# Re-placing the side work of an interleaved attention loop, and the bank pairs of the shared feed-forward

## The chip, the cores and the metric

The kernel is one decoder layer written in Bass for one NeuronCore of a Trainium2 chip. It runs on one core. The metric is the device time of one execution in microseconds. Every engine (TensorE, called PE in the profile; VectorE, DVE; ScalarE, ACT; GpSimd, POOL; SyncE, SP) has a program of its own, in a fixed order written out by hand, and the five programs meet only at semaphores.

## The reference

Input is `x` (16 batches, 128 tokens, 256 features) and a context of the same shape. Three residual blocks follow each other:

```
x = x + attn(layernorm(x))          # differential attention, 16 heads x 2 halves of 8, two softmaxes, o = a1 - lam*a2,
                                    # rms norm over each head's 16 values, times subln_w, @ W_proj + b_proj
x = x + xattn(layernorm(x), ctx)    # softmax((q Wq+bq)/8 . (ctx Wk+bk)) @ (ctx Wv+bv), @ Wf + bf, gelu, + ctx
x = x + ffn(layernorm(x))           # shared: (silu(x w1) * (x w2)) w3, hidden 1024
                                    # routed: sigmoid router, top 2 of 16 experts of hidden 256, gates times outputs
```

All of it is float32; only the attention's scores use three-part bfloat16 splits.

## The kernel before, in words

The 16 batches are four chunks of four (`NC = 4`, `CB = 4`). The program has these stages:

- **Head.** Loads, the first layernorm, and `qk`/`values` of chunks 0 and 1. Queries and keys are split into three bfloat16 parts (`put_first` on ACT, `subtract_first` on DVE, `put_second` on ACT, `put_third` on POOL), stored to HBM by `store_part`, and fetched back in packed form by `fetch`.
- **The attention loop**, `STEPS = 32` steps of two halves `(s, a)`. A half is, on PE: `exps(s, a)` (8 matmuls, line 428, banks 2 and 3), `scores(s + 3, a)` (8 matmuls, line 407, banks 0 and 1), one `pv` (line 440, bank 4), in the second half also `turn_max(s + 2)` (line 415, bank 5), and then `between(s, a)`. DVE takes the maximum of the scores (`max_of`, line 875), and once a step turns the outputs (line 882) and takes reciprocals (line 886). ACT does the exponentials (line 1348) and copies the turned maxima (line 1341). POOL splits the maxima (`split_max`, lines 1589 to 1595) and combines the outputs (`combine`, lines 1604 to 1613). SP sends the maxima into the query tile (`put_max`, line 1790); `exps(s, 0)` waits for that transfer (`m_put`).
- **Pieces between the halves.** Everything else that can be done early is hung into the loop by tables that name a half `(s, a)`: `qk` and `values` of chunks 2 and 3, the folding of the cross attention's weights (WF, A, B, M), the turned context, keys and values of the cross attention (CTX, KEYS, U), the attention's output projection with its norm (CLIP, SQUARE, SUM, ROOT, NORM, OT, OUT, ADD), the next layernorm (STATS, SCALE, NORMAL, ROWS), and the cross attention of chunks 0 and 1 (SCORES, MAX, EXP, TURN_P, WEIGH, FO). Each engine's own `between` looks its part up in the tables. The pieces share PSUM banks 6 and 7, so a piece waits until the one before it in its bank has been read.
- **After the loop.** Cross attention of chunks 2 and 3 among the first `up`s of the shared feed-forward; `up(c, f)` computes 128 hidden columns of gates and ups for chunk c (line 612), `silu_up` and `gate_up` make `hTs`, and `down(c, j)` multiplies by `W3s` (line 623). Routing (`route`) runs on DVE in between: `chosen_both`, a matmul that ranks, `slotted`. POOL then scatters the rows to expert slots (line 1729).
- **Experts.** 47 tiles (`turn_x`, `raise_`, `lower`), rows scattered back by line 1632.
- **End.** The shared `up`s 2 to 7 of chunk 3, the routed rows added (lines 1132, 1135), `down(3, j)`, and the output.

The order on SP is fixed as well: in step s it does `put_max(s + 2)`, then the packed fetches, stores and context loads of that step. SP waits at each instruction in turn.

## Time and profile before

| | us |
|---|---|
| median of 3 runs | 595.57 (593.27 to 596.82) |
| the profiled execution, time | 595.6 |
| its span, first to last instruction | 594.4 |
| PE busy in the span | 541.0 (91%) |
| DVE busy | 311.4 (52%) |
| ACT busy | 261.2 (44%) |
| POOL busy | 229.5 (39%) |
| mean granted TensorE clock | 0.974 of full speed |

The profiled execution lies at the median of the runs; 1.2 us of its time lie outside the span. A row of a timeline is: start, duration, engine, line, operation, what it writes and reads, count, and in brackets how long the engine stood idle before it and what ended that. PE's granted clock falls after idle stretches, and then the same matmuls take about twice as long.

### The profile page before, as it was taken

How to read it: one execution, taken by the hardware profiler on the slowest of the kernel's cores; microseconds unless marked ns; L12 is line 12 of the kernel's file. 1: busy time of each engine (PE TensorE's matmuls, PEld its weight loads, DVE VectorE, ACT ScalarE, POOL GpSimd, SP SyncE). 2: the span in 40 equal slices, each digit the busy share in tenths (PEclk: the TensorE clock that was granted, in tenths of full speed). 3: DMA queues.
4: the chain of work that ended last, by engine and by line, in shares of the span. 5: the costliest groups of instructions: out<-in, count | busy, mean ns of one | idle time of the engine just before them, and what ended most of it. 6: DMA issues, size and time to landing. Idle time of an engine off the chain costs nothing.

```text
span 594.4 us, 10885 instructions
## 1 busy us (share of the span) xinstructions
PE 541.0 (91%) x3792; PEld 372.6 (63%) x3792; DVE 311.4 (52%) x677; ACT 261.2 (44%) x420; POOL 229.5 (39%) x473
## 2 busy tenths in 40 slices
PE   8968879689887879899999899999999999999888
PEld 6544435355544544665685457456999999999347
DVE  5867865957796797896242752111222222222184
ACT  6326555444562554835412200201666666665110
POOL 2534775635553554422010004563243334443100
PEclk9989998989897999999999989999999999999899
DMA  7892562713222141990029906222233333332552
GB/s 241 230 204 74 152 193 78 229 53 112 81 67 74 42 145 59 150 285 1 0 71 350 288 0 195 90 89 71 73 91 94 95 93 96 91 90 76 198 187 72
DMA packets 62197, 72.46 MB, mean 122 GB/s; under 512 B 14816, under 2 KB 55264, under 8 KB 60608
## 3 DMA queue, kind: packets, MB, share of 16 engines
q1 hardware_dynamic: 58160, 60.59, 36.0%
q0 software_dynamic: 3792, 10.39, 5.0%
q10 hardware_dynamic: 192, 0.79, 0.6%
q8 instruction: 32, 0.52, 0.4%
q14 instruction: 21, 0.17, 0.1%
HBM read 45.32 MB, written 26.03 MB: 120 GB/s over the span
## 4 chain that ended last, share of the span: by engine, by line
PE 49%; issue 18%; DVE 13%; POOL 10%; DMA 5%; ACT 3%; SPq 2%; POOLq 0%; DVEq 0%; ACTq 0%
PE ps L612 17%; PE ps L623 9%; POOL y_rows L1632 7%; DVE nmax L875 3%; PE ps L539 3%; PE ps L440 2%; PE ps L376 2%; PE ps L389 2%; PE ps L428 2%; DVE OT L882 2%; PE ps L407 2%; PE ps L505 2%; PE ps L520 2%; POOL goes_to L1626 1%; PE ps L632 1%
## 5 line engine op out<-in xcount | busy, mean ns | idle before, releaser
L875 DVE TENSOR_REDUCE nmax<-ps 128x8 f32<-128x1024 f32 x64 | 77.7, 1215 | 43.4 <-PE ps L407 39.4
L668 PE MATMUL ps<-xt,Wn 128*128 128x128 f32 x752 | 91.8, 275 | 0.3 <-ACT xt L1450 0.3
L668 PEld LDWEIGHTS ps<-xt,Wn 128*128 128x128 f32 x752 | 87.7, 192 | 0.6 <-ACT xt L1450 0.5
L1348 ACT ACTIVATE prob<-ps 128x1024 f32<-128x1024 f32 x64 | 65.5, 1023 | 35.9 <-PE ps L428 35.9
L1632 POOL DMA_INDIRECT y_rows<-yo,goes_to x47 | 46.0, 978 | 81.8 <-DVE yo L1129 81.5
L1443 ACT ACTIVATE sil<-ps 128x512 f32<-128x512 f32 x32 | 19.1, 597 | 122.1 <-PE ps L612 119.3
L1121 DVE TENSOR_TENSOR ht<-sa,ps 128x256 f32<-128x256 f32 x47 | 19.8, 421 | 99.2 <-PE ps L679 95.2
L612 PE MATMUL ps<-xT,W1s 128*128 128x512 f32 x128 | 63.7, 622 | 3.5 <-DVE yo L1129 1.9
L623 PE MATMUL ps<-W3s,hTs 128*128 128x256 f32 x256 | 56.5, 381 | 4.4 <-DVE hTs L1052 4.4
L612 PE MATMUL ps<-xT,W2s 128*128 128x512 f32 x128 | 60.3, 593 | 0.0
L1052 DVE TENSOR_TENSOR hTs<-sil,ps 128x512 f32<-128x512 f32 x32 | 21.9, 686 | 70.1 <-PE ps L612 66.0
L623 PEld LDWEIGHTS ps<-W3s,hTs 128*128 128x128 f32 x256 | 48.2, 190 | 14.0 <-DVE hTs L1052 5.9
L1729 POOL DMA_INDIRECT x_slots<-XN,slot_i x32 | 31.9, 996 | 62.3 <-DVE slot_i L1102 43.1
L1463 ACT ACTIVATE Wn<-W 128x1024 f32 x47 | 49.7, 1057 | 12.6 <-issue 12.6
L679 PE MATMUL ps<-W,ht 128*128 x188 | 48.3, 380 | 0.2 <-DVE yo L1129 0.2
L440 PE MATMUL ps<-prob,Vp 128*32 128x256 f32 x512 | 42.2, 402 | 4.0 <-DVE OT L882 2.8
L612 PEld LDWEIGHTS ps<-xT,W2s 128*128 128x128 f32 x128 | 24.5, 192 | 31.6 <-issue 30.2
L612 PEld LDWEIGHTS ps<-xT,W1s 128*128 128x128 f32 x128 | 24.3, 197 | 29.1 <-issue 25.6
L428 PEld LDWEIGHTS ps<-pack_q,pack_k 51*128 51x128 bf16 x512 | 15.1, 95 | 36.4 <-issue 25.9
L1604 POOL TENSOR_SCALAR rden<-rden,neg_lam 128x8 f32<-128x8 f32 x32 | 11.9, 371 | 67.3 <-DVE rden L886 67.3
L428 PE MATMUL ps<-pack_q,pack_k 51*128 51x128 bf16 x512 | 26.1, 222 | 10.8 <-ACT prob L1348 7.7
L407 PE MATMUL ps<-pack_k,pack_q 48*128 48x128 bf16 x512 | 25.9, 221 | 10.8 <-DVE nmax L875 6.5
(186 smaller groups left out, 854.6 us busy)
## 6 DMA issues: line engine op xcount, KB each, us to landing
W<-in_L_ffn_routed_w_dram SPq DMA_DIRECT2D x12, 1024.0 KB
pack_q<-qk_parts SPq DMA_DIRECT2D x48, 128.0 KB, 3.1
xg<-x_slots SPq DMA_DIRECT2D x47, 129.0 KB
x_slots<-zero SPq DMA_DIRECT2D x11, 512.0 KB, 10.3
pack_k<-qk_parts SPq DMA_DIRECT2D x42, 128.0 KB, 3.1
qk_parts<-part SPq DMA_DIRECT2D x21, 256.0 KB, 3.1
yg<-y_rows SPq DMA_DIRECT2D x4, 1024.0 KB, 8.6
X<-in_x_dram SPq DMA_DIRECT2D x4, 512.0 KB, 7.0
```

What stands on the lines that cost most here:

```text
L407: r = t.matmul(ps[:, b + m, h * P:(h + 1) * P], Qp[u][rr, 4 * a + h, lo:lo + P], Kp[u][rr, 4 * a + h, lo:lo + P], start=True, stop=True, t ...
L428: r = t.matmul(ps[:, 2 + m, h * P:(h + 1) * P], Kp[u][rr, 4 * a + h, lo:lo + P], Qp[u][rr, 4 * a + h, lo:lo + P], start=True, stop=True, t ...
L440: r = t.matmul(ps[VP * h:VP * (h + 1), 4, a * 2 * P:(a + 1) * 2 * P], Vp[:, s // CS % 2, s % CB, s // CB % 2 * HU + 4 * a + h, :], prob[:, ...
L612: r = t.matmul(ps[:, up_bank(c, f) + i, :], w[:, k, f * P:(f + 1) * P], xT3[c][:, k, :], start=(k == 0), stop=(k == KT - 1))
L623: r = t.matmul(ps[:, 2 + j % 2, 0:D], hTs[:, f, j * P:(j + 1) * P], W3s[:, f, :], start=(f == 0), stop=(f == FS - 1))
L668: r = t.matmul(ps[:, 2 + p, h * P:(h + 1) * P], Wn[:, n % 3, k, h * P:(h + 1) * P], xt[:, p, k, :], start=(k == 0), stop=(k == KT - 1))
L679: r = t.matmul(ps[:, 6 + p, 0:D], ht[:, p, k, :], W3[:, ds(e, 1), k, :].rearrange("p o f -> p (o f)"), start=(k == 0), stop=(k == KT - 1))
L875: v.tensor_reduce(nmax[:, s % 4, a, :, :], ps[:, b:b + 2, :].rearrange("p m (h t) -> p m h t", h=4), AX_X, ALU.max, negate=True).then_inc( ...
L1348: a.activation(prob[:, n:n + 2, :], ps[:, 2:4, :], ACT.Exp, scale=HD ** -0.5).then_inc(exped, 1)
L1463: a.activation(Wn[:, n % 3, :, :].rearrange("p k f -> p (k f)"), W12[:, ds(e, 1), :, :].rearrange("p o k f -> p (o k f)"), ACT.Copy).then_ ...
L1632: g.indirect_dma_start(out=y_rows, out_offset=bass.IndirectOffsetOnAxis(ap=goes_to[:, n:n + 1].bitcast(U32), axis=0), in_=yo[:, p, :], in_ ...
L1729: g.indirect_dma_start(out=x_slots, out_offset=bass.IndirectOffsetOnAxis(ap=slot_i[:, i, b:b + 1].bitcast(U32), axis=0), in_=XN[:, b, :], ...
```

## The change

All of the tables that place pieces are new. Several pieces are divided in two or four: `root_o` (2 parts to 4), `norm_o`, `turn_attn`, `add_o`, `stats` and `put_fo` (1 to 2 each). `project_values(2, i)` moves from behind the loop into it. The first two `values(1, i)` come before the first `scores`, and DVE takes six maxima in a row. The load of context chunk 1 goes to a tile of its own (`Cx1`, over weights no longer needed), no longer waits for the stores of chunk 3, and is loaded a second time at step 16 for the residual. On SP, a context load now comes ahead of `put_max` of its step; the eight loads of `Wp` are split over steps 5 and 6. Each piece waits for the reader of its bank that the new tables make the last one. In the shared feed-forward, chunks 2 and 3 use two pairs of banks in turn, one `up` of the next chunk goes ahead of each chunk's `down`s, one `up` goes ahead of the ranking matmuls, and the last `up`s no longer wait for the last expert tile's output (`y_put`) but for its input (`xt_put`).

```diff
-TURN_AT = (2, 1)
-QK_AT = ((3, 0), (4, 0), (5, 0), (6, 0))
-VALUES_AT = {2: ((8, 0), (8, 1)), 3: ((16, 0), (16, 1))}
-WF_AT, A_AT, B_AT, M_AT = (1, 0), (1, 1), (7, 0), (7, 1)
-CTX_AT = {0: (9, 1), 1: (11, 1), 2: (17, 0), 3: (28, 0)}
+STATS3_AT, SCALE3_AT, NORM3_AT, TURN_AT = (0, 0), 0, (1, 1), (2, 0)
+QK_AT = ((3, 0), (4, 0), (7, 0), (9, 0))
+VALUES_AT = {2: ((9, 1), (11, 0)), 3: ((18, 1), (19, 1))}
+WF_AT, A_AT, B_AT, M_AT, PUT_B_AT, WP_AT = (5, 0), (1, 0), (10, 0), (8, 0), (11, 1), (9, 0)
+CTX_AT = {0: (12, 0), 1: (12, 1), 2: (20, 0), 3: (26, 0)}
...
-STATS_AT = {0: (14, 1), 1: (23, 0), 2: (31, 0)}
-SCALE_AT = {0: 15, 1: 23, 2: 31}
-CONTEXT_AT = {0: 17, 1: 25}
-CTX_LOAD_AT = {0: 4, 1: 10, 2: 12, 3: 16}
+STATS_AT = {0: ((16, 1), (18, 0)), 1: ((24, 0), (24, 1)), 2: ((30, 1), (31, 0))}
+SCALE_AT = {0: 18, 1: 25, 2: 29}
+CONTEXT_AT = {0: (29, 29, 29, 29), 1: (30, 30, 31, 31)}
+CTX_LOAD_AT = {0: 4, 1: 11, 2: 15, 3: 20}
+CTX1_AGAIN_AT = 16
...
         def up_bank(c, f):
-            return 4 if c == NC - 1 and f < AHEAD else 0
+            if c == NC - 1:
+                return 4 if f < AHEAD or f % 2 else 0
+            return 4 if c == NC - 2 and f % 2 == 0 else 0
+
+        def down_bank(c, j):
+            return 2 + j if c == NC - 1 else 2 + j % 2
...
+            for i in range(2):
+                values(1, i)
             scores(0, 0)
-            values(1, 0)
             scores(0, 1)
-            values(1, 1)
+            turn(norm, 2, 4, xn)
             scores(1, 0)
-            turn(norm, 2, 4, xn)
...
-            for i in range(2):
-                project_values(2, i, 6 + i)
             t.wait_ge(o_turned, STEPS)
...
-            for f in (3, 4, 5):
+            for f in (3, 4, 5, 6):
                 up(1, f)
             t.wait_ge(chosen_both, 1)
...
-            t.wait_ge(y_put, NT)
+            t.wait_ge(xt_put, NT)
             for f in range(AHEAD, FS):
                 up(NC - 1, f)
...
             for s in range(STEPS):
+                for c in range(NC):
+                    if s == CTX_LOAD_AT[c]:
+                        if c == 1:
+                            q.wait_ge(a_made, 1)
+                            q.wait_ge(b_made, 1)
...
+                        fetch_context(c)
                 if s + LEAD - 1 < STEPS:
                     put_max(s + LEAD - 1)
```

On PE, just ahead of the loop, the order before was as follows (L407 are the first scores, L389 `values(1, i)`, L362 the turn of chunk 2, L415 `turn_max`, L376 `qk(2, i)`, L428 the first `exps`):

```order
L407 MATMUL ps<-pack_k_81,pack_q_78 128x128 x8
L389 MATMUL ps<-Wv__95,xT 128x256 x4
L407 MATMUL ps<-pack_k_81,pack_q_78 128x128 x8
L389 MATMUL ps<-Wv__95,xT 128x256 x4
L407 MATMUL ps<-pack_k_81,pack_q_78 128x128 x8
L362 MATMUL ps<-ident,xn 128x128 x8
L407 MATMUL ps<-pack_k_81,pack_q_78 128x128 x8
L415 MATMUL ps<-identb,mpart 128x128
L407 MATMUL ps<-pack_k_81,pack_q_78 128x128 x8
L376 MATMUL ps<-xT_99,Wqk 128x512 x2
```

The same place on PE in the changed kernel (L416 are `values`, L434 scores, L381 the turn, L442 `turn_max`, L399 `qk`):

```order
L416 MATMUL ps<-Wv__95,xT 128x256 x8
L434 MATMUL ps<-pack_k_81,pack_q_78 128x128 x16
L381 MATMUL ps<-ident,xn 128x128 x8
L434 MATMUL ps<-pack_k_81,pack_q_78 128x128 x8
L442 MATMUL ps<-identb,mpart 128x128
L434 MATMUL ps<-pack_k_81,pack_q_78 128x128 x8
L399 MATMUL ps<-xT_99,Wqk 128x512 x2
```

Both `values` now stand ahead of the first scores, and the first two scores follow each other.

On SP, steps 4 to 6 of the loop before (the packed fetches read `qk_parts`, the stores write it, `mT` is `put_max`):

```order
L1790 DMA pack_q_79<-mT 3x8x128 x2
L1782 DMA pack_q_78<-qk_parts 16x4096 x4
L1758 DMA qk_parts<-part_108 128x2x512 x4
L1794 DMA Cx<-in_ctx_dram 128x4x256
L1790 DMA pack_q_79<-mT 3x8x128 x2
L1782 DMA pack_q_78<-qk_parts 16x4096 x2
L1782 DMA pack_k_81<-qk_parts 16x4096 x2
L1790 DMA pack_q_80<-mT 3x8x128 x2
L1782 DMA pack_k_81<-qk_parts 16x4096 x4
```

And SP in steps 4 to 6 of the changed kernel:

```order
L1897 DMA Cx<-in_ctx_dram 128x4x256
L1893 DMA pack_q_79<-mT 3x8x128 x2
L1885 DMA pack_q_78<-qk_parts 16x4096 x4
L1861 DMA qk_parts<-part_108 128x2x512 x4
L1893 DMA pack_q_79<-mT 3x8x128 x2
L1885 DMA pack_q_78<-qk_parts 16x4096 x2
L1885 DMA pack_k_81<-qk_parts 16x4096 x2
L1853 DMA Wp<-in_L_attn_W_proj_dram 16x2x256 x4
L1893 DMA pack_q_80<-mT 3x8x128 x2
L1885 DMA pack_k_81<-qk_parts 16x4096 x4
L1853 DMA Wp<-in_L_attn_W_proj_dram 16x2x256 x4
```

The context load went from behind the stores to the front, and the `Wp` loads came into these steps.

On POOL, the end of the loop before, from the last `split_max` (`rden`, `o` and `Ob` are one `combine`, `y` the layernorm's scale, `sq` the clip):

```order
L1595 TENSOR_TENSOR mpart<-mrest,mpart 128x2x2x4
L1604 TENSOR_SCALAR rden<-rden,neg_lam 128x2x4
L1607 TENSOR_TENSOR o_92<-OT,rden 128x128 x2
L1613 TENSOR_TENSOR Ob<-o_92 128x2x4x16
L1604 TENSOR_SCALAR rden<-rden,neg_lam 128x2x4
L1607 TENSOR_TENSOR o_92<-OT,rden 128x128 x2
L1613 TENSOR_TENSOR Ob<-o_92 128x2x4x16
L1604 TENSOR_SCALAR rden<-rden,neg_lam 128x2x4
L1607 TENSOR_TENSOR o_92<-OT,rden 128x128 x2
L1613 TENSOR_TENSOR Ob<-o_92 128x2x4x16
L1568 TENSOR_SCALAR y<-mv 128x4
L1570 TENSOR_TENSOR y<-y,minus_half 128x4
```

And POOL at the end of the changed loop, from the `combine` of step 28:

```order
L1701 TENSOR_SCALAR rden<-rden,neg_lam 128x2x4
L1704 TENSOR_TENSOR o_92<-OT,rden 128x128 x2
L1710 TENSOR_TENSOR Ob<-o_92 128x2x4x16
L1665 TENSOR_SCALAR y<-mv 128x4
L1667 TENSOR_TENSOR y<-y,minus_half 128x4
L1738 TENSOR_TENSOR X<-X,Cx 128x256 x4
L1701 TENSOR_SCALAR rden<-rden,neg_lam 128x2x4
L1704 TENSOR_TENSOR o_92<-OT,rden 128x128 x2
L1710 TENSOR_TENSOR Ob<-o_92 128x2x4x16
L1738 TENSOR_TENSOR X<-X,Cx 128x256 x2
```

The scale, which needs DVE's statistics of step 31, and the context additions now stand ahead of the `combine`s of steps 29 to 31.

## Rows read from the trace of the kernel before

**Rows 1.** Stages (the windows view): stretch, length, busy of each engine, PEclk, DMA.
```profile
49.26:100.84 51.58, 45.65 (x515) 24.83 (x515) 37.22 (x57) 30.25 (x48) 34.46 (x82) 0.97 0.45 136
100.84:242.09 141.25, 117.00 (x1318) 67.51 (x1317) 108.61 (x195) 72.78 (x116) 71.84 (x200) 0.94 0.36 95
242.09:254.61 12.52, 10.95 (x68) 9.57 (x64) 11.69 (x30) 9.89 (x22) 5.88 (x10) 1.00 1.06 207
```
**Rows 2.** Timeline of PE: one half with a piece, one without, the next `exps`.
```profile
75.14 0.40 PE L428 MATMUL ps<-pack_q,pack_k 51*128 51x128 bf16 x8 [0.92 <-ACT prob L1348]
76.27 1.99 PE L376 MATMUL ps<-xT,Wqk 128*128 128x512 f32 x4
78.18 0.40 PE L428 MATMUL ps<-pack_q,pack_k 51*128 51x128 bf16 x8
80.46 0.40 PE L428 MATMUL ps<-pack_q,pack_k 51*128 51x128 bf16 x8 [0.93 <-ACT prob L1348]
```
**Rows 3.** The page's group of the loop's exponentials on ACT.
```profile
L1348 ACT ACTIVATE prob<-ps 128x1024 f32<-128x1024 f32 x64 | 65.5, 1023 | 35.9 <-PE ps L428 35.9
```
**Rows 4.** Timeline of PE, three long waits in the loop.
```profile
87.06 0.40 PE L428 MATMUL ps<-pack_q,pack_k 51*128 51x128 bf16 x8 [2.20 <-DMA pack_q<-mT]
120.56 1.97 PE L496 MATMUL ps<-ident,Cx 128*128 128x128 f32 x8 [4.63 <-DMA Cx<-in_ctx_dram]
150.26 0.40 PE L407 MATMUL ps<-pack_k,pack_q 48*128 48x128 bf16 x8 [1.30 <-DVE nmax L875]
```
**Rows 5.** Timeline of PE: the first scores, the first `exps`.
```profile
34.66 0.40 PE L407 MATMUL ps<-pack_k,pack_q 48*128 48x128 bf16 x8 [4.09 <-DMA pack_q<-qk_parts]
49.26 0.40 PE L428 MATMUL ps<-pack_q,pack_k 51*128 51x128 bf16 x8 [0.72 <-DMA pack_q<-mT]
```
**Rows 6.** Timeline of SP's queue.
```profile
46.34 4.46 SPq L1790 DMA_DIRECT2D pack_q<-mT  x4
76.77 2.69 SPq L1782 DMA_DIRECT2D pack_q<-qk_parts  x4
82.72 1.59 SPq L1790 DMA_DIRECT2D pack_q<-mT  x2
94.70 3.68 SPq L1750 DMA_DIRECT2D Wp<-in_L_attn_W_proj_dram  x8
```
**Rows 7.** Timeline of POOL at the loop's end, and one context addition.
```profile
215.48 0.72 POOL L1639 TENSOR_TENSOR X<-X,Cx 128x256 f32<-128x256 f32 x1
243.64 0.32 POOL L1604 TENSOR_SCALAR rden<-rden,neg_lam 128x8 f32<-128x8 f32 x1
245.48 1.56 POOL L1621 TENSOR_SCALAR sq<-Ob 128x1024 f32<-128x1024 f32 x1
```
**Rows 8.** Timeline of PE in the shared feed-forward.
```profile
341.51 0.70 PE L788 MATMUL ps<-both,earlier 128*128 128x256 f32 x2 [2.22 <-DVE before L1081]
352.29 14.08 PE L623 MATMUL ps<-W3s,hTs 128*128 128x256 f32 x64 [0.88 <-DVE hTs L1052]
```
**Rows 9.** The chain of waits, the eight `up`s of chunk 2: start, us, what.
```profile
366.37 27.48 PE ps L612 x64
```
**Rows 10.** Timelines of DVE, POOL and PE: routing, and the first expert tile.
```profile
354.18 0.17 DVE L1102 CAST slot_i<-top 128x16 int32<-128x16 f32 x1
412.28 0.19 POOL L1626 CAST goes_to<-xg 128x1 int32<-128x1 f32 x1 [3.69 <-DMA xg<-x_slots]
415.47 0.60 PE L657 MATMUL ps<-ident,xg 128*128 128x128 f32 x4
```
**Rows 11.** Timelines of PE and SP's queue at the end.
```profile
553.74 3.64 PE L612 MATMUL ps<-xT,W1s 128*128 128x512 f32 x4 [1.87 <-DVE yo L1129]
556.38 2.27 SPq L1906 DMA_DIRECT2D yg<-y_rows  x4
577.98 14.08 PE L623 MATMUL ps<-W3s,hTs 128*128 128x256 f32 x64 [1.68 <-DVE hTs L1052]
```
**Rows 12.** The tile view of `yg`: its DMA from issue to landing.
```profile
DMA to landing us min/median/max: 5.2/8.6/11.8
```

More of the change, by code:

```diff
@@ L501, in project_keys @@
                 t.wait_ge(cT_put, 2 * (c + 1))
-                if c == 2 and e:
-                    t.wait_ge(kT_put, KT * 2 + 1)
+                if c == 0 and e == 0:
+                    t.wait_ge(a_put, 1)
+                if (c, e) == (0, 0):
+                    t.wait_ge(cT_put, 4)
+                if (c, e) == (1, 0):
+                    t.wait_ge(x_added, 1)
+                if (c, e) == (1, 1):
+                    t.wait_ge(cT_put, 6)
+                if (c, e) == (2, 0):
+                    t.wait_ge(norm.put, 10)
+                if (c, e) == (2, 1):
+                    t.wait_ge(u_put, 4)
                 for k in range(KT):
@@ L605, in up @@
                 n = FS * c + f
+                left = n - 1 if c >= NC - 2 and (c, f) != (NC - 1, 1) else n
                 if f == 0:
@@ L700, in tensor_program @@
                 qk(1, i)
+            for i in range(2):
+                values(1, i)
             scores(0, 0)
-            values(1, 0)
             scores(0, 1)
-            values(1, 1)
+            turn(norm, 2, 4, xn)
             scores(1, 0)
-            turn(norm, 2, 4, xn)
-            scores(1, 1)
             t.wait_ge(identb_made, 1)
@@ L712, in tensor_program @@
             turn_max(0)
+            scores(1, 1)
+            qk(2, 0)
             scores(2, 0)
-            qk(2, 0)
+            turn_max(1)
             scores(2, 1)
-            turn_max(1)
             qk(2, 1)
@@ L772, in tensor_program @@
             t.wait_ge(u_put, 2 * NC)
-            down(0, 0)
             weigh_values(3)
             route_logits(2)
-            for j in range(1, CB):
+            for j in range(CB):
                 down(0, j)
@@ L1209, in vector_program @@
             root_o(0)
+            root_o(1)
             gate_up(0, 0)
-            root_o(1)
+            root_o(2)
+            root_o(3)
             put_logits(0)
-            norm_o(NC - 1)
-            turn_attn(NC - 1)
+            for i in range(2):
+                norm_o(NC - 1, i)
+            for i in range(2):
+                turn_attn(NC - 1, i)
             gate_up(0, 1)
             normalize(norm3, 1, 1, rows(XN, 1))
-            put_fo(2)
-            add_o(NC - 1, 4)
+            for i in range(2):
+                put_fo(2, i)
+            for i in range(2):
+                add_o(NC - 1, i)
             v.wait_ge(x_added, 2 * NC)
@@ L1233, in vector_program @@
             gate_up(0, 7)
-            put_fo(3)
+            for i in range(2):
+                put_fo(3, i)
             put_logits(2)
@@ L1649, in between @@
                     put_third(2, 3)
-                if (s - 1, 0) in QK_AT:
-                    put_third(3, QK_AT.index((s - 1, 0)))
+                for i in range(4):
+                    if s == THIRD_AT[i]:
+                        put_third(3, i)
                 for c in range(NC - 1):
@@ L1854, in sync_program @@
                         store_part(2, i)
-                if s == 7:
-                    for j in range(4):
+                if s in (5, 6):
+                    for j in (0, 1) if s == 5 else (2, 3):
                         for i in range(2):
```

448 lines of the change are left out of this document (263 added, 185 removed).

## The prediction

> **What bounds the kernel now.** I read the slices of the page first (PE near nine tenths all the way, with dips between 50 and 250 us), then the windows of the stages, then PE's timeline half by half, and for every idle stretch of PE its releaser on DVE, SP and POOL. The stages are in [rows 1]: steps 0 to 8 of the loop take 51.58 us with PE busy 45.65, steps 9 to 31 take 141.25 with PE busy 117.00 at a granted clock of 0.94, the way from the loop to the first shared `up` 12.52. So PE bounds the loop, but not tightly: about 30 us of the loop are PE idle, and more is lost because the matmuls behind an idle stretch run at the lower of the two clock levels. DVE is busy 108.61 of the 141.25, unevenly.
>
> An ordinary half is in [rows 2]. From `exps` to piece 1.13 us (75.14 to 76.27), the piece 1.91, so 3.04 in all. The half without a piece lasted 2.28 with 0.93 of PE idle, since the next `exps` need the exponential out of banks 2 and 3. That takes 1.02 [rows 3]; with 0.4 for `exps` and what is between them an empty half costs at least about 1.6 on an even course. A piece in an otherwise empty half is therefore nearly half free, and a half in which DVE has more than PE is lost.
>
> The long waits are in [rows 4]: 2.20 for the maxima's transfer, 4.63 for context chunk 1, 1.30 for a late maximum; three more of 1.35, 1.19 and 0.98 are of the same kind.
>
> **Part 1, ahead of the loop.** PE stands 4.09 us until the packed queries land at 34.66 [rows 5], and then does two `values` of 1.9 us between the first scores, which makes DVE's six maxima wait. After the change both `values` fit into the 4.09. Then the chain is DVE's: six maxima of 1.22 in a row with one late score give about 43.9, the two `qk` end at 44.1. The first maxima's transfer can be issued at about 39.3; in [rows 6, 5] from issue (46.34) to the first `exps` (49.26) it is 2.9, so 42.2, not late. `exps` at 44.1 instead of 49.26: **-5.2** (bounds -3, if `turn_max` is late by a piece, and -6).
>
> **Part 2, steps 0 to 8.** For every half I added up what stands there on PE, DVE and ACT at these durations, and took the largest, or 1.6. Before, 13 pieces lie in these steps and the sum is 47.8, against 51.58 measured. After, 9 pieces lie there and the sum is 42.1. But SP does not get shorter. In steps 4 to 6 of the new order stand, between one `put_max` and the next, a fetch of 2.69, stores and context load, which took until 82.72 together [rows 6], and now half of the `Wp` loads (3.68 for eight) twice: 6.5, 5.9 and 5.9 us of issue, while the halves of steps 5 and 6 ask for only 3.2 to 3.6 a step. Following the queue through: the transfer for step 7 is issued some 6.5 us after that for step 6 and lands 2.9 to 4.3 later (4.3 is 82.72 to 87.06 in [rows 6, 4]), so `exps(7, 0)` waits 2.5 to 3.9, and steps 4, 5, 6, 8 and 9 some 0.5 to 1.3 each. I take 5.1 for all: 47.2, **-4.4** (bounds -9.5, no backlog, and -1).
>
> What the page on DMA says bears on this. The Trainium skill ("DMA: Bandwidth & Descriptors", section "Issuing engines are not separate DMA queues") has it that the time a sequencer takes to initiate a DMA is usually small beside the DMA. Here it is not: four issues took 2.69 us [rows 6]. By that rule there would be no backlog and this part would be worth the -9.5 that stand above as a bound.
>
> **Part 3, steps 9 to 31.** Same sum: before 134.2 with 32 pieces, after 128.2 with 38, because the loads that DVE has beyond PE's in its heavy halves fall from 21.6 to 7.5 us (norm, transposition, root, sums and `put_fo` divided, layernorm later). Before, 141.25 less the six long waits and their slow matmuls (about 16.3) leaves 125.0, so 43% of DVE's surplus was absorbed by neighbours; after, by the same share, 128.2 - 3.2 = 125.0. The context load for chunk 1 is now issued behind a `put_max`, a fetch and stores of step 10, some 5.7 us into step 11, and needs 4.1; its piece stands 8.2 us in: a wait of 1.5 and a few slow matmuls, +2.0, in place of 4.63 and some. Each added wait on a bank I followed to its reader: it stands a half or more ahead, so nothing for those; +3.0 for what such a count does not see. 130.0, **-11.3** (bounds -16 and -5). Two `project_values` are in this sum.
>
> **Part 4, from the loop to the first `up`.** This gets longer. POOL's scale of chunk 2 is placed at step 29 but needs DVE's statistics of step 31. Behind it on POOL stand four context additions of 0.72 [rows 7], the `combine` of step 29 (1.65), two additions, a `combine`, two more, and the `combine` of step 31. DVE's last turn of the outputs waits for the `combine` of step 29. Counted from the end of the statistics: scale 1.4, additions to 4.3, `combine` to 6.0, so the last turn starts at 6.0 and the normalisation of chunk 2 at 7.0; before it came at 1.5. The last `pv` ends at 3.1, and PE, whose `project_values` are gone from here, stands idle about 4 us. The clip (1.56, [rows 7]) ends at 13.8 and the first `up` starts at about 19.1, so 16.0 after the last `pv` against 12.52 [rows 1]; the matmuls behind the idle stretches add 1.5. **+5.0** (bounds 0 and +8).
>
> **Part 5, feed-forward.** Each `up` takes 3.43 (27.48 for eight, [rows 9]). PE waits 2.22 for `chosen_both` and then runs the ranking and an `up` slowly [rows 8]: from 339.1 to 366.2 it takes 27.1 for two `up`s, 1.0 of ranking and 14.08 of `down`, which is 21.9. With an `up` ahead of the ranking and one ahead of the `down`s, all 5.2 go; the waits of 0.88 and 0.94 for `hTs` go likewise at the next two chunk ends: 0.85 and 0.94. The two bank pairs themselves are worth nothing between these: 27.48 for eight is PE without a gap. Is the first tile there? Slot numbers are ready at 354.35 and the tile has landed at 412.3, needed at 415.47 [rows 10]. Slots come 4.4 us earlier, since DVE no longer waits behind slow `up`s; the tile then lands 1.7 before PE comes, 6.0 earlier than before. At the end PE waits 1.87 for the last output copy and then runs slowly (3.64, full speed 1.9) [rows 11]; both go, 3.6. The routed rows land 5.2 us after the issue at 556.38 at the earliest [rows 12], by 561.6; DVE needs them from 562.9, has eight additions ahead of the last `hTs` instead of eleven, and the wait of 1.68 [rows 11] falls to 0.8. Together 0.9 + 6.0 + 4.6: **-11.5** (bounds -12.5 and -7).
>
> **Sum.** -5.2 - 4.4 - 11.3 + 5.0 - 11.5 = -27.4. From the span of 594.4 that is 567.0, and with the 1.2 us outside it **568.2** against 595.6 of the profiled execution, which is the median of the runs.
>
> **Rivals.**
> - *SP's backlog does not bite, or the tail is short* (parts 2 or 4 at their good bound): 568 - 5 = 563. For it: before, with 95% of these issues in the same order, only one wait of 2.20 is seen. Against: those steps lasted 4.6 to 5.4 us then. 18%.
> - *SP's queue holds the loop further on*: late landings of 4.3 us throughout, the context chunk 1 behind them, parts 2 and 3 at -1 and -7: 568 + 8 = 576. For it: the fetches, stores and second context load are all still there in less time. 22%.
> - *The tile chain takes the feed-forward's gain*: if the scatter is not earlier, PE waits for the first tile at step six of its gain, part 5 is -7: 573. 8%.
> - *Slower than before*, by one mechanism, the clock in steps 9 to 31: if each of the many small waits leaves PE at the lower level, a piece costs about 3.6 to 3.7 instead of 1.9 (the ratio in [rows 11]). From about 16 of the 38 pieces at that level the 27 us are used up; all give 568 + 67. Before, about five pieces ran so, each behind a wait of over a microsecond. 4%, at about 600.
> - *The gain is not there*, since the pieces only swap waits: within 0.5%, 3%.
>
> **Chances and range.** My forecast, between 564 and 573, has 45%. The 8-in-10 range goes from the good rival's lower side to the bad one's upper: **558 to 582**. Within 0.5% (3 us) cannot be told from no change here. Faster 0.93, same 0.03, slower 0.04.
>
> **What would show it.** Part 1: first `exps` at 43 to 46. Part 2: a wait of 2 us or more for the maxima's transfer at `exps(7, 0)`, step 9 at 90 to 93. Part 3: the wait for context chunk 1 down to 1 to 2 us, PE's clock in the stage above 0.96. Part 4: POOL's context additions directly behind the scale, PE idle some 4 us, 15 to 18 us from the last `pv` to the first `up`. Part 5: no wait at the ranking, and `up`s directly behind the last `lower`. The prediction is wrong if the loop is not at least 10 us shorter, or if new waits on bank readers add up to over 5 us.

## The result, and the profile after

The changed kernel takes **567.8 us** (median of 4 runs, 566.11 to 569.25) against 594.42 (4 runs) of the kernel before beside it: ratio 0.956, 95% interval 0.949 to 0.964. Forecast was 568.2. Its profiled execution took 569.25, the slowest of the four, with a span of 568.0; the stages below are of that one execution.

The windows view cut at the same places as [rows 1] (first `exps`, step 9, last `pv`, first `up`, first expert tile, last `lower`), the columns as there, without the experts' 136.4 us, which are the same in both; first the changed kernel:

```profile
46.20:94.22 48.02, 40.56 (x482) 20.35 (x481) 36.53 (x55) 29.05 (x45) 31.59 (x82) 0.93 0.48 146
94.22:223.89 129.67, 122.72 (x1365) 73.67 (x1365) 107.87 (x199) 75.48 (x122) 69.07 (x192) 0.97 0.44 110
223.89:240.56 16.67, 10.46 (x50) 8.75 (x49) 13.88 (x34) 7.82 (x19) 11.48 (x21) 0.80 1.11 292
240.56:393.80 153.24, 152.35 (x558) 96.00 (x559) 64.94 (x175) 38.33 (x61) 43.72 (x57) 1.00 0.37 119
...
530.18:568.00 37.82, 34.67 (x112) 20.84 (x111) 20.32 (x43) 3.58 (x6) 1.91 (x2) 1.00 0.50 177
```

and the two stages of the kernel before that answer to its last two:

```profile
254.61:415.47 160.86, 155.07 (x558) 96.54 (x559) 65.03 (x174) 38.34 (x61) 44.72 (x58) 0.99 0.41 129
...
551.86:594.40 42.54, 36.65 (x113) 21.70 (x112) 20.24 (x43) 3.59 (x6) 1.92 (x2) 0.96 0.44 158
```

| stretch | before | forecast | after | moved (forecast) |
|---|---|---|---|---|
| start to first `exps` | 49.26 | 44.1 | 46.20 | -3.1 (-5.2) |
| steps 0 to 8 | 51.58 | 47.2 | 48.02 | -3.6 (-4.4) |
| steps 9 to 31 | 141.25 | 130.0 | 129.67 | -11.6 (-11.3) |
| last `pv` to first `up` | 12.52 | 17.5 | 16.67 | +4.2 (+5.0) |
| first `up` to first tile | 160.86 | 154.0 | 153.24 | -7.6 (-6.9) |
| experts | 136.39 | 136.4 | 136.38 | 0 |
| last `lower` to the end | 42.54 | 37.9 | 37.82 | -4.7 (-4.6) |
| span | 594.40 | 567.0 | 568.00 | -26.4 (-27.4) |

What PE waits for in the changed kernel, from the list of waits (us in all, times, longest):

```profile
PE ps L455 <- DMA pack_q<-mT: 4.8, 5, 1.7
...
PE ps L381 <- DVE xn L920: 4.6, 1, 4.6
PE ps L529 <- DMA Cx<-in_ctx_dram: 2.1, 1, 2.1
PE ps L442 <- POOL mpart L1692: 1.9, 1, 1.9
```

Of the three long waits of [rows 4] shorter ones are left: the context chunk's wait is 2.1 for 4.63. Two are new. The maxima's transfer is late five times (four of them, at steps 6 to 9, are the backlog of part 2; the fifth, 1.12, is at step 17), and 4.6 us are lost in one place behind the loop (part 4). The last row is one that the forecast lacks, in the head; PE's timeline there:

```profile
38.27 0.27 PE L442 MATMUL ps<-identb,mpart 128*128 128x128 bf16 x1 [1.93 <-POOL mpart L1692]
39.01 3.78 PE L399 MATMUL ps<-xT,Wqk 128*128 128x512 f32 x4
44.02 2.25 PE L399 MATMUL ps<-xT,Wqk 128*128 128x512 f32 x4
46.20 0.40 PE L455 MATMUL ps<-pack_q,pack_k 51*128 51x128 bf16 x8
```

The gap of 4.09 of [rows 5] is gone, but `turn_max(0)` waits 1.93 us for POOL's split of the maxima, and the `qk` behind it runs at half speed, 3.78 for 1.98. The wait and the half speed are two things, as run 2 shows below: with the same wait of 1.93 its matmuls stay at full speed, and its first `exps` come at 43.50.

SP's queue in steps 4 to 6 (`put_max` is L1893, fetch L1885, stores L1861, `Wp` L1853), which answers to [rows 6]:

```profile
72.18 1.47 SPq L1893 DMA_DIRECT2D pack_q<-mT  x2
73.76 2.45 SPq L1885 DMA_DIRECT2D pack_q<-qk_parts  x4
76.25 2.19 SPq L1861 DMA_DIRECT2D qk_parts<-part  x4
78.49 1.60 SPq L1893 DMA_DIRECT2D pack_q<-mT  x2
...
82.67 2.44 SPq L1853 DMA_DIRECT2D Wp<-in_L_attn_W_proj_dram  x4
85.16 1.60 SPq L1893 DMA_DIRECT2D pack_q<-mT  x2
```

From one `put_max` to the next are 6.3 and 6.7 us; 6.5 and 5.9 were forecast. Behind the loop, on POOL, DVE and PE:

```profile
220.76 0.23 POOL L1665 TENSOR_SCALAR y<-mv 128x4 f32<-128x4 f32 x1 [11.16 <-DVE mv L908]
222.08 2.77 POOL L1738 TENSOR_TENSOR X<-X,Cx 128x256 f32<-128x256 f32 x4
```
```profile
224.96 0.18 DVE L1119 RECIPROCAL den<-den 128x4 f32<-128x4 f32 x1 [4.29 <-POOL X L1738]
226.75 0.70 DVE L956 STREAM_TRANSPOSE OT<-ps 128x512 f32<-128x512 f32 x1
227.92 1.83 DVE L920 TENSOR_SCALAR xn<-X,mv,y 128x256 f32<-128x256 f32 x4 [0.18 <-issue]
```
```profile
228.48 2.02 PE L381 MATMUL ps<-ident,xn 128*128 128x128 f32 x8 [4.59 <-DVE xn L920]
240.56 1.98 PE L671 MATMUL ps<-xT,W1s 128*128 128x512 f32 x4 [0.74 <-ACT xT L1397]
```

POOL waits 11.16 us in the scale, then does four context additions before its next `combine`. The normalisation starts 7.25 us after the statistics (220.67); 7.0 was counted.

In the feed-forward the waits of [rows 8] and the first wait of [rows 11] are gone: the ranking stands directly behind an `up`, the last `up`s directly behind the last `lower`, and of 1.68 ahead of the last `down`s 0.85 is left.

```profile
327.32 0.59 PE L857 MATMUL ps<-both,earlier 128*128 128x256 f32 x2
530.01 1.88 PE L671 MATMUL ps<-xT,W1s 128*128 128x512 f32 x4
551.62 14.08 PE L682 MATMUL ps<-W3s,hTs 128*128 128x256 f32 x64 [0.85 <-DVE hTs L1141]
```

### The profile page after: what moved, and what is told of

It is laid out like the page before. It is cut to its first block, busy times and chain, and to the rows that moved or that the text cites. A ratio compares the mean times of both kernels' runs of the same rounds, so it can differ in the third digit from the quotient of the medians.

```text
span 568.0 us, 10919 instructions
## 1 busy us (share of the span) xinstructions
PE 537.7 (95%) x3792; PEld 374.1 (66%) x3792; DVE 311.8 (55%) x685; ACT 260.1 (46%) x420; POOL 228.0 (40%) x473
## 4 chain that ended last, share of the span: by engine, by line
PE 80%; DVE 6%; SPq 5%; ACT 3%; issue 3%; DMA 2%; POOL 1%; ACTq 0%; DVEq 0%; POOLq 0%
PE ps L671 18%; PE ps L739 15%; PE ps L682 10%; PE ps L750 7%; PE ps L399 5%; PE ps L467 3%; PE ps L595 3%; PE ps L416 2%; PE ps L455 2%; PE ps L572 2%; PE ps L548 2%; SPq L1885 2%; DVE nmax L949 2%; PE ps L695 2%; PE ps L728 2%
## 5 line engine op out<-in xcount | busy, mean ns | idle before, releaser
L739 PE MATMUL ps<-xt,Wn 128*128 128x128 f32 x752 | 91.8, 275 | 0.1
L671 PE MATMUL ps<-xT,W1s 128*128 128x512 f32 x128 | 60.6, 596 | 1.6 <-ACT sil L1542 0.9
L399 PE MATMUL ps<-xT,Wqk 128*128 128x512 f32 x64 | 34.6, 684 | 1.6 <-ACT xT L1397 1.6
L750 PEld LDWEIGHTS ps<-W,ht 128*128 128x128 f32 x188 | 32.2, 191 | 3.1 <-issue 0.6
```

The source lines that it names most:

```text
L399: r = t.matmul(ps[:, qk_bank(c, i), :], Wqk[:, k, f, :, :].rearrange("p d m -> p (d m)"), xT_of(c)[:, k, :], start=(k == 0), stop=(k == KT ...
L671: r = t.matmul(ps[:, up_bank(c, f) + i, :], w[:, k, f * P:(f + 1) * P], xT3[c][:, k, :], start=(k == 0), stop=(k == KT - 1))
L739: r = t.matmul(ps[:, 2 + p, h * P:(h + 1) * P], Wn[:, n % 3, k, h * P:(h + 1) * P], xt[:, p, k, :], start=(k == 0), stop=(k == KT - 1))
L750: r = t.matmul(ps[:, 6 + p, 0:D], ht[:, p, k, :], W3[:, ds(e, 1), k, :].rearrange("p o f -> p (o f)"), start=(k == 0), stop=(k == KT - 1))
```

## The experiments

Each run's time is a median beside runs of the kernel before on its chip; since these differ a little from chip to chip (591.6 to 594.8), the ratio is the better measure. The changed kernel has 0.956 (0.949 to 0.964). Where times lie closer than about 3 us, the profiles are compared stage by stage. But a profile is one execution, and it too varies where an edit changes nothing: over the profiles of kernels with the changed kernel's loop from step 9 on (runs 1 to 4 and the changed kernel), steps 9 to 31 take 125.6 to 129.7 us; over those with its loop end, the way from the last `pv` to the first `up` takes 16.1 to 17.6.

**1. The feed-forward of the kernel before in the changed kernel** (`e1_ffn_before`).

```diff
-            for f in (3, 4, 5, 6):
+            for f in (3, 4, 5):
                 up(1, f)
...
-            up(1, 7)
-            up(2, 0)
+            for f in (6, 7):
+                up(1, f)
             for j in range(CB):
                 down(1, j)
...
-            t.wait_ge(xt_put, NT)
+            t.wait_ge(y_put, NT)
```

> The changed kernel with the shared feed-forward of the kernel before (order of ups and downs, one bank pair per up, the wait for the last output copy, the spread of the routed additions). My theory (part 5, all of it comes from matmuls put beside the waits): the waits for chosen_both, for hTs at two chunk ends and for the last output copy come back with their slow matmuls, 153.2 us from the first up to the first expert tile become 160.9, 37.8 us behind the last lower become 42.5, in all +12.3: about 580. Rival (the gain came from somewhere else, as transfers that no longer collide with the feed-forward's start): the stretches stay within 2 us of the changed kernel's, 568 to 571.

579.21 us, ratio 0.976 (0.971 to 0.981): +11.4. The windows of the two stretches:

```profile
238.71:398.38 159.67, 154.84 (x558) 96.41 (x559) 65.37 (x176) 38.32 (x61) 44.59 (x58) 0.99 0.37 118
535.07:577.50 42.43, 36.64 (x112) 21.70 (x112) 20.23 (x43) 3.58 (x6) 1.91 (x2) 0.96 0.45 158
```

The waits are back at their old size (2.21 at the ranking, 0.88, 0.85, 1.87, 1.68) and with them 6.4 + 4.6 us. That the gain of part 5 lies in this block is shown; the run puts the whole block back, so what each move in it is worth is read from its wait and was not tried singly. The missing 0.9 of the 12.3 is the wait of 0.94 for `hTs` of chunk 0, which did not come back. It stands ahead of this block: the changed kernel also has `weigh_values(3)` and `route_logits(2)` ahead of `down(0, 0)`, where the kernel before had them behind it, and this run leaves that as it is.

**2. SP's queue: the loads of `Wp` ahead of the loop** (`e4_wp_in_head`); the block of steps 5 and 6 moves ahead of `store_part(1, 0)`.

```diff
+            for j in range(4):
+                for i in range(2):
+                    load(Wp[...], W_proj..., head_weights_in)
             store_part(1, 0)
...
-                if s in (5, 6):
-                    (the same loads)
```

> The changed kernel with the eight loads of the projection's weights issued ahead of the loop (where SP's queue has 3.8 us free, 27.6 to 31.4) and not in steps 5 and 6. Theory (SP's issue time is what makes the maxima's transfers late in steps 6 to 9): the waits of 0.83, 0.79, 0.41 and 1.68 us before the exps of steps 6 to 9 shrink to under 1 in all, the slow matmuls behind them (1.1, 1.5, 1.5 us over full speed in steps 6, 7 and 9) go, steps 0 to 8 take 43.5 to 45 instead of 48.0: 563 to 565. Rival (the transfers are late because of their flight, 2.9 to 4.3 us, whatever is ahead of them in the queue): the waits stay above 3 us in all and the time within 1 us of 567.8.

566.28 us, ratio 0.953 (0.949 to 0.958), short of the 563 to 565 forecast. Step 9 starts at 91.83 instead of 94.22, since the wait of 1.68 there is gone. In the eight profiles with the changed kernel's list on SP for steps 0 to 9 it starts between 93.5 and 95.8, so this run is outside them and the `Wp` loads cost step 9 some 2 to 4 us. The stage itself is no shorter (48.33), as the loop began at 43.50. That earlier start does not come from the edit, which leaves PE's order in the head as it was: the wait is the same, only the matmuls behind it are fast.

```profile
38.10 0.22 PE L442 MATMUL ps<-identb,mpart 128*128 128x128 bf16 x1 [1.93 <-POOL mpart L1692]
38.57 1.98 PE L399 MATMUL ps<-xT,Wqk 128*128 128x512 f32 x4
43.50 0.40 PE L455 MATMUL ps<-pack_q,pack_k 51*128 51x128 bf16 x8
```

The largest wait is now at step 7:

```profile
71.32 3.15 SPq L1885 DMA_DIRECT2D pack_q<-qk_parts  x4
74.51 2.20 SPq L1861 DMA_DIRECT2D qk_parts<-part  x4
76.76 1.60 SPq L1893 DMA_DIRECT2D pack_q<-mT  x2
```
```profile
79.64 0.61 PE L455 MATMUL ps<-pack_q,pack_k 51*128 51x128 bf16 x8 [2.16 <-DMA pack_q<-mT]
```

The transfer for step 7 stands behind a fetch and four stores, not behind `Wp`. So `Wp` costs at step 9, and the stores of step 4 at step 7.

**3. Both `qk` of chunk 2 ahead of `turn_max`** (`e5_qk_first`).

```diff
+            qk(2, 0)
             turn_max(0)
             scores(1, 1)
-            qk(2, 0)
             scores(2, 0)
+            qk(2, 1)
             turn_max(1)
             scores(2, 1)
-            qk(2, 1)
```

> The changed kernel with both query-key projections of chunk 2 ahead of the transposition of the maxima that they followed, in the head. Theory (the head came out 2.1 us longer than forecast because PE waits 1.93 us for the first maxima and both projections behind that wait run at the lower clock level, 3.78 and 2.25 us instead of 1.98): the wait falls below 0.5, the projections take 2.0 each, first exps at 42.5 to 43.5 instead of 46.2, the rest unchanged: about 565. Rival (the maxima's chain on DVE and the transfer's flight set the first exps): first exps not before 45.5, the time within 1 us of 567.8.

569.13 us, ratio 0.958 (0.953 to 0.963). The wait is gone and the projections take 1.96 and 1.98, as the theory has it, but the whole gains nothing:

```profile
43.29 0.40 PE L455 MATMUL ps<-pack_q,pack_k 51*128 51x128 bf16 x8 [1.41 <-DVE nmax L949]
```
```profile
43.29:94.85 51.56, 43.29 (x481) 21.30 (x483) 36.99 (x55) 28.82 (x44) 31.23 (x82) 0.87 0.49 146
```

First `exps` 2.9 us earlier, at 43.29, but step 9 at 94.85: nothing of it is left. All four profiles with this order have their first `exps` at 43.2 to 43.5, behind a wait of 1.41 for a maximum of DVE; the nine with the old order have the wait of 1.93 to 1.94 and lie anywhere from 43.5 to 46.5. So the edit buys an even start, and against the best case of the old order almost nothing. Over the eight profiles of kernels with this list on SP for steps 0 to 9, the first `exps` lie between 43.3 and 46.5 and step 9 between 93.5 and 95.8, and the one that begins first is not the one that arrives first. In the changed kernel SP's queue is full from 57.4 to 97.5 us but for one gap of 0.4, so it sets step 9. Its length is not fixed, however: the 52 issues from `put_max(3)` to `put_max(9)` took 34.0 us in the changed kernel and 36.7 in this run, where four single issues lasted 1.19 to 1.63 instead of the usual 0.4 to 0.9; the other six lie between. What makes an issue long stays open.

**4. SP's list evened** (`e9_sp_even`, and `e10_sp_even_qk` with the edit of 3 as well).

```diff
-                if s in (3, 4):
-                    for i in ((0,), (1, 2))[s - 3]:
-                        store_part(2, i)
+                if s == 3:
+                    store_part(2, 0)
+                if s == 7:
+                    for i in (1, 2):
+                        store_part(2, i)
```

> The changed kernel with the projection's weights loaded ahead of the loop and the second and third parts of chunk 2's split stored at step 7 of SP's program instead of step 4 (four issues of 2.2 us; step 7 has none else). The runs so far have step 9 at 94 to 95 us whether the loop starts at 43.3 or at 46.2, and at 91.8 without the weights' loads. Theory (SP's queue, full without a gap from step 3 to step 7, sets the time of step 9, and the stores of step 4 are what makes the transfer for step 7 late): the waits before the exps of steps 6 to 9 fall below 1 us in all, step 9 at 87.5 to 90, the time 561 to 564. Rival (what is late is the transfer's own flight of 4 us while other transfers are on the way): waits of 2 us and more stay at steps 6 or 7, step 9 not before 91.5, the time within 1 us of the 566.3 measured with the weights moved alone.

> The same, and both query-key projections of chunk 2 ahead of the transpositions of the maxima in the head, which alone brought the first exps to 43.3 and the whole nothing (569.1 against 567.8). Theory (that gain was given back at SP's queue): with the queue relieved it stays, and the time is another 1 to 2 us under the run without it. Rival (the order of the head gives nothing whatever the queue is, because the idle time only moves to the wait for the maxima): within 0.7 us of that run.

563.92 (0.950, 0.945 to 0.955) and 562.72 (0.951, 0.946 to 0.956), on the same chip. Step 9 comes at 91.72 and 90.03, and steps 0 to 8 take 46.6 in both profiles, for 48.0. The waits for transfers at steps 7 to 9 are gone, as the theory has it. In these two profiles the earlier start of the second (43.47 for 45.15) is still there at step 9; but the first is of the slowest of its four executions and the second of the fastest, and the medians (1.2 apart, each with a spread of 4.6 or more) do not settle whether the head's order gains anything. The first is later at step 9 than the 87.5 to 90 I expected, and hardly earlier than in run 2, because at step 6 the rival is right: there the transfer leaves right behind a context load, and `exps` starts 4.3 us after its issue:

```profile
71.86 0.47 SPq L1897 DMA_DIRECT2D Cx<-in_ctx_dram  x1
72.38 1.48 SPq L1893 DMA_DIRECT2D pack_q<-mT  x2
```
```profile
76.72 0.61 PE L455 MATMUL ps<-pack_q,pack_k 51*128 51x128 bf16 x8 [2.23 <-DMA pack_q<-mT]
```

**5. The scale of chunk 2 at step 31** (`e2_scale_31`).

```diff
-SCALE_AT = {0: 18, 1: 25, 2: 29}
+SCALE_AT = {0: 18, 1: 25, 2: 31}
```

> The changed kernel with POOL's scale of chunk 2 at step 31 instead of 29, nothing else. In the changed kernel it waits 11.16 us on POOL for DVE's statistics of step 31, and four context additions, a combine, and on DVE the outputs put_fo(1) (whose buffer lies over chunk 0's context) and the last turn are late behind it; PE idles 4.59. Theory of the prediction, part 4 (the scale is what blocks POOL): the additions move ahead of the statistics, put_fo(1) starts as its matmuls end (223.3 counted in the changed kernel's time), the normalisation 2 us earlier, PE idle 2.6 and the first up 14 to 15 us after the last pv instead of 16.7: 565 to 566. Rival (DVE's own order sets the normalisation, the outputs and the last turn ahead of it): under 0.7 us of change in that stretch.

565.95 us, ratio 0.955 (0.950 to 0.960). The medians cannot tell this from the changed kernel, the profile can: PE waits 2.00 instead of 4.59, and the first `up` comes 14.52 us after the last `pv` instead of 16.67, where the kernels with the old placing have 16.1 to 17.6. That is as reckoned: what blocks POOL is the scale.

```profile
223.83 1.99 PE L381 MATMUL ps<-ident,xn 128*128 128x128 f32 x8 [2.00 <-DVE xn L920]
```

**6. The loop's end reordered** (`e11_tail`): context additions at steps 21 to 28, the scale of chunk 2 at step 30, and on DVE

```diff
+            normalize(norm, NC + 2, 2, xn)
+            for i in range(2):
+                put_fo(1, i)
             turn_o(STEPS - 1)
             invert(STEPS - 1)
-            normalize(norm, NC + 2, 2, xn)
             add_cross(0)
```

and on PE `project_values(3, i)` ahead of `cross_scores(2)`.

> The changed kernel with its loop end reordered: context additions at steps 21 to 24, 27 and 28, scale of chunk 2 at step 30, on DVE the normalisation of chunk 2 ahead of the outputs and the last turn, on PE the last project_values ahead of the cross scores. Theory (PE's idle 4.6 us and the slow matmuls behind it come from this order, not from a lack of work): xn is there when the last pv ends, the wait of 4.59 falls below 0.5, the first up comes 10.5 to 12 us after the last pv instead of 16.7: 562 to 563. Rival (POOL's combine of step 31, the clip and the scale of the next normalisation hold the first up at the same time after the loop): PE idles later in the same stretch instead, the first up not before 14.5 us, the time not under 565.5.

571.07 us, ratio 0.963 (0.958 to 0.967): slower than the changed kernel. The theory is wrong. The rival's numbers came in (first `up` 15.89 us after the last `pv`, PE idle later in the same stretch), but not for its reason:

```profile
228.00 1.11 PE L381 MATMUL ps<-ident,xn 128*128 128x128 f32 x8 [2.57 <-DVE OT L956]
228.93 5.30 PE L572 MATMUL ps<-M_T,cT 128*128 128x256 f32 x16
...
238.80 1.84 PE L381 MATMUL ps<-ident,XN 128*128 128x128 f32 x8 [2.78 <-DVE XN L920]
```

`xn` is ready in time, but the turn goes into the outputs' bank and so waits for DVE's last turn, which I had put behind the outputs; and DVE's queue has `max_cross` ahead of the next normalisation, so the cross scores, moved back behind `project_values(3, i)`, hold it up. The stretch is even 0.8 shorter than in the changed kernel; what is lost in this profile lies in steps 0 to 8 (49.2 for 48.0, within what this list on SP shows elsewhere) and behind the first `up`, whose matmuls are slow here (first `up` to first tile 155.5 for 153.2).

**7. The load of context chunk 1 at step 10** (`e7_ctx1_at_10`), one number in `CTX_LOAD_AT`, **and the roots of chunk 0 earlier as well** (`e12_roots_earlier`).

```diff
-ROOT_AT = {0: ((10, 1), (11, 0), (12, 1), (12, 1)), ...
+ROOT_AT = {0: ((10, 1), (11, 0), (11, 0), (12, 0)), ...
...
-CTX_LOAD_AT = {0: 4, 1: 11, ...
+CTX_LOAD_AT = {0: 4, 1: 10, ...
```

> The changed kernel with the load of context chunk 1 one step earlier in SP's program (step 10 for 11). Theory (the load is late only because of what is queued ahead of it: a fetch of 2.4 and stores of 1.6 us): it is issued at about 105.5 instead of 112.6, the wait of 2.10 us at its piece goes and with it at most 1 us of slow matmuls: 565 to 566, steps 9 to 31 in 127 instead of 129.7. Rival (another wait takes its place at once, as the next maxima's transfer that now stands behind it): the time within 1 us of 567.8.

> The changed kernel with the load of context chunk 1 at step 10, as in the run that gave 567.5 and a new wait of 1.72 us for a maximum at step 13, and the last two parts of chunk 0's root one half earlier (the steps 11 and 12, first halves, for 12, second). In both traces six operations of that root (128x64, two inputs) took up to 1.08 us instead of 0.23 while POOL's additions and the last thirds of the split (128x512, 1.15 each) ran beside them. Theory (DVE and POOL hold each other up there, and that makes the maximum late): away from the thirds the operations take 0.23, the wait of 1.72 falls below 0.5, steps 9 to 31 take 124.5 to 126: 564 to 565.5. Rival (the maximum is late because DVE has too much there at any speed): the wait stays over 1 us and the time within 1 us of 567.5.

567.47 (0.956, 0.951 to 0.960) and 565.24 (0.954, 0.946 to 0.961). The first removes the wait of 2.1 and gets one of 1.72 at step 13 in its place. The median is the rival's, and so is the exchange of one wait for another, though the new one is for a maximum of DVE and not for the maxima's transfer. Steps 9 to 31 take 126.7 and 126.4 in the two profiles; kernels with an unchanged loop have that too (126.2 in run 3), so no gain of either edit is shown. What makes the maximum late is to be seen in DVE's and POOL's timelines of the changed kernel:

```profile
110.36 0.23 DVE L1026 SCALAR_TENSOR_TENSOR yo__56<-newton,yo__56 128x64 f32<-128x64 f32 x1
116.54 1.08 DVE L1026 SCALAR_TENSOR_TENSOR yo__56<-newton,yo__56 128x64 f32<-128x64 f32 x1
117.65 1.08 DVE L1024 TENSOR_TENSOR newton<-yo__56 128x64 f32<-128x64 f32 x1
```
```profile
116.39 2.27 POOL L1678 TENSOR_TENSOR part<-rest,part 128x512 bf16<-128x512 f32 x2
```

The same operation takes 0.23 alone and 1.08 beside POOL's third of the split, and each slow one ends within 0.1 us of one of POOL's two. With the roots moved away from there the slowest of these operations takes 0.50, and the wait of 1.72 is gone, but another of 1.16 us for a maximum stands one and a half steps earlier, where the roots are now. So the contention is shown; what it is worth in time is not resolved between these two medians.

The Trainium skill ("SBUF — State Buffer", section "SBUF: two separate sides") says that DVE and GpSimd share a port pair which a DVE instruction with two inputs in SBUF needs too, against a GpSimd instruction that reads SBUF, and that whichever starts first holds it for its whole instruction. By that a short operation of DVE with two inputs lasts until POOL's beside it ends; the trace agrees, 1.08 beside 1.15.

**8. DVE's divided loads joined again** (`e6_undivided`), PE's order unchanged.

```diff
-NORM_AT = {0: ((13, 1), (14, 0)), 1: ((21, 1), (22, 1)), ...
+NORM_AT = {0: ((14, 0), (14, 0)), 1: ((22, 1), (22, 1)), ...
...
```

> The changed kernel with DVE's divided loads of the loop standing together again (root in two places per chunk instead of four or three, normalisation, transposition, additions of chunk 0 and statistics each in one), the order on PE unchanged. Counted half by half as in part 3, the largest of PE, DVE, ACT and 1.6 us sums to 129.9 instead of 128.2 in steps 9 to 31, and DVE's surplus over PE to 9.6 us instead of 7.5. Theory (a half in which DVE has more than PE is lost, about 57% of it): 1 to 2 us more in that stage, 568.5 to 570. Rival (dividing the loads gave nothing, the buffers of three steps between DVE and PE swallow them): within 0.7 us of 567.8; a second one (DVE bound much more closely than the count says): 572 or more.

569.44 us, ratio 0.958 (0.951 to 0.965), +1.6 in the middle of what the count gave, but inside the noise. The trace has three new waits for maxima behind the joined loads (0.91, 0.79 and 0.84 us), the kind that [rows 4] shows at 150.26. But the stage where the theory puts its 1 to 2 us is not longer, 129.19 against 129.67:

```profile
95.75:224.94 129.19, 122.01 (x1365) 72.93 (x1365) 107.66 (x199) 76.28 (x123) 70.68 (x193) 0.99 0.45 110
```

The changed kernel's own profile has two waits of over 1 us there that this one lacks (2.10 for the context, 1.12 for a transfer). So dividing the loads removes these waits for maxima, but that it saves time is not shown; nor does the time settle the second rival's 572: the median speaks against it, but the upper end of the ratio's interval (0.965) is above it.

**9. Together** (`e13_together`, then `e14_together_2` after its trace): the edits of 2 to 5 and 7, with DVE's order `normalize, turn_o, invert, put_fo(1)` behind the loop; the second time the context loads apart from the fetches, besides stores and root parts moved as its expectation lists.

```diff
-CTX_LOAD_AT = {0: 7, 1: 10, 2: 15, 3: 20}
+CTX_LOAD_AT = {0: 7, 1: -1, 2: 17, 3: 20}
...
                     put_max(s + LEAD - 1)
+                if s == 10:
+                    (wait for a_made and b_made)
+                    fetch_context(1)
```

> All together: the projection's weights ahead of the loop; all stores of chunk 2's parts and the first context load at step 7 of SP's program; both query-key projections ahead of the maxima in the head; context chunk 1 loaded at step 10; the root of chunk 0 earlier; scale of chunk 2 at step 31; on DVE the normalisation of chunk 2 ahead of the last turn, and the outputs behind it. Theory (these are separate waits of PE): first exps 43.4, step 9 at 87 to 89, steps 9 to 31 124 to 126, first up 11 to 13 us after the last pv, the rest as in the changed kernel: 552 to 557. Rival (each wait removed gives place to the next, DVE's queue now bounding the loop): the sum falls short by a third or more, 558 to 562.

> The combined kernel (558.2) with SP's list evened further, from its own trace: its waits of 2.00 us for the maxima at step 12 and 0.96 at step 17 stand behind a context load, fetches and stores queued in one step. Now the first context load alone stays with the four stores of step 7 (three stores go back to step 3), context chunk 1 is issued behind the maxima of step 10, the stores of chunk 3's parts at steps 11 and 15, which have no fetch, context chunk 2 at step 17; the first two parts of chunk 0's root one half earlier. Theory (SP's bursts are still what ends last in steps 9 to 17): both waits under 0.7 us, the loop 2 to 4 us shorter, 554 to 556.5. Rival (the burst only moves, and another wait of the same size takes its place): within 1 us of 558.2 or above.

558.22 us, ratio 0.940 (0.933 to 0.946), then **554.97 us** (6 runs), ratio 0.936 (0.931 to 0.941), which beats both kernels. The first fell short by the rival's measure, in steps 9 to 31 (129.1 for the 124 to 126 forecast). The largest wait there is not DVE's, as the rival had it, but again one of SP's list:

```profile
100.05 1.65 SPq L1899 DMA_DIRECT2D Cx<-in_ctx_dram  x1
101.75 1.58 SPq L1895 DMA_DIRECT2D pack_q<-mT  x2
```
```profile
105.08 0.52 PE L455 MATMUL ps<-pack_q,pack_k 51*128 51x128 bf16 x8 [2.00 <-DMA pack_q<-mT]
```

The second has this wait no more. Its stages, from first `exps` to first `up`:

```profile
43.39:87.36 43.97, 38.05 (x482) 19.44 (x483) 36.89 (x55) 28.06 (x44) 30.62 (x82) 1.00 0.50 149
87.36:212.05 124.69, 119.53 (x1365) 71.90 (x1365) 106.89 (x202) 75.96 (x123) 77.43 (x206) 1.00 0.47 119
212.05:224.72 12.67, 7.99 (x49) 6.42 (x49) 12.29 (x31) 7.82 (x19) 4.16 (x8) 1.00 1.11 274
```

Against the changed kernel's: 4.0, 5.0 and 4.0 us less, and the granted clock is 1.00 throughout, where it was 0.93, 0.97 and 0.80. PE has the same matmuls and is busy 2.5, 3.2 and 2.5 us less: between these two profiles, 8.2 of the 13.0 us were matmuls at the lower level, and the rest waits. (They are the slowest of the changed kernel's four executions and the second fastest of this one's six; the medians are 12.8 us apart in all, the profiled times 15.9.)

## Why the prediction was right

The total was 0.4 us off, and that close a hit is luck: two terms together came 3.0 us short, three were 1.9 better than forecast, and the profiled execution whose stages are compared lies 1.45 us above the median. What the runs bear out is the mechanism of parts 4 and 5, and for part 2 the queue; part 3 came out as forecast but rests on the traces alone. Step by step:

1. **The head: mis-sized, -3.1 for -5.2.** "Both `values` fit into the 4.09" is what the trace shows. The step that failed is "one late score ... the two `qk` end at 44.1": `turn_max(0)` stands ahead of both `qk` and waits 1.93 for POOL's split, and the `qk` take 3.78 and 2.25. The wait alone costs little, since run 2 has it too and starts the loop at 43.50; what the term lacks is the half speed that follows it in most profiles, up to 3 us. Run 3 puts the `qk` first, has no such wait there and gets first `exps` at 43.3.
2. **Steps 0 to 8: the mechanism was right, its place only partly.** The queue's issue times were as counted, 6.3 to 6.7 us for 5.9 to 6.5. The waits came at steps 6, 7, 8 and 9 (0.83, 0.79, 0.41, 1.68) and not mainly as 2.5 to 3.9 at `exps(7, 0)`; PE itself was later there. I put the new backlog down to the `Wp` loads; run 2 shows that these cost step 9 some 2 to 4 us, and that step 7 waits for the four stores of step 4, which were there before. A fault behind the size: terms 1 and 2 were added as if independent. With SP full, a head that is shorter was paid back at step 9 (all of it in run 3), so they are one term, -6.6 measured against -9.6. By the rule of the Trainium skill that I weighed there, issues would cost next to nothing. Here one issue takes 0.4 to 0.9 us and a fetch lands about 3 us after its issue, so six of them in a row take longer to issue than one takes to land. In steps 0 to 8 runs 2, 4 and 9 moved only issues on SP, and step 9 came at 91.8, then 91.7 and 90.0, then 87.4 (steps 0 to 8 in 44.0 for 48.0), so the rule does not hold here.
3. **Steps 9 to 31: right, -11.6 for -11.3.** The context wait is 2.1 for 1.5 expected; the two longest waits for maxima went; PE is busy 122.72 for 117.00 with six more pieces, two `project_values` among them, at a clock of 0.97 for 0.94. The count half by half (the largest of PE, DVE, ACT and 1.6) gave 130.0. Profiles of kernels with the same loop spread from 125.6 to 129.7, though, so a hit within 0.3 us is partly chance. Run 8, made to test the share of 57% that I took from the kernel before, does not show it: the stage was not longer with DVE's surplus back. That share stays argued. No run puts the old tables of these steps back either, so that the new placing is what gave the 11.6 rests on the waits gone from the trace and on PE's clock, not on a run of its own.
4. **The loop's end: right, +4.2 for +5.0,** with the wait (4.59 for "about 4"), and the start of the normalisation (7.25 for 7.0) as counted. Run 5 confirms the scale as the blocker. One thing was not in my account: DVE's outputs of chunk 1 go into a buffer that lies over chunk 0's context, so they wait for POOL's additions too (4.29, above), and end at 226.8, where the `combine` that I named ends at 226.5. Either alone would give the same time.
5. **Feed-forward: right, -12.3 for -11.5.** Run 1 gives it back wait by wait. One reading was wrong: the wait of 0.94 lies at the end of chunk 0, at 298.41 in the kernel before and thus ahead of the ranking, so no `up` put ahead of `down`s removed it. It went by `weigh_values(3)` and `route_logits(2)`, which now stand ahead of `down(0, 0)`. That the two bank pairs as such are worth nothing was argued and not tried alone.

The rival of SP's queue (22%) came in for steps 0 to 8 alone. With the head, terms 1 and 2 are 3.0 short together; the others, 0.3 to 0.8 better than their terms each, made up for most of it. The rival of the clock in steps 9 to 31 did not happen: it rose there from 0.94 to 0.97.

## What to carry to other kernels

Count the issuing queue like an engine: here eight DMA issues of 0.6 us each between two that PE waits for bounded a stage, and in run 3 a gain ahead of it was handed back there. A load moved to where PE is free still has to be looked up on the other four engines and in the buffers it shares, since a one-number move (the scale two steps early) cost 2 us by blocking what was queued behind it. And where a change removes several short waits, price them with the matmuls behind them: between the profiles of the changed and of the last kernel these were 8.2 of 13.0 us. Last, compare a profile with the spread of the profiles in which nothing was changed at that place; in run 8 that turns a supported theory into an open one.
